# Moving a square root, eight scalings and four gathers in GpSimd's order

## The chip, the cores and the metric

The kernel runs on one core of a Trainium2 chip. Its time is the device time of one execution in microseconds (us). The engines are called PE (TensorE), DVE (VectorE), ACT (ScalarE), POOL (GpSimd) and SP (SyncE, which issues most DMAs). They run side by side and wait for one another by semaphores.

## The reference

One layer of a language model on `x` of 8 x 256 tokens with 256 features: `x + attention(layernorm(x)) + experts(layernorm(x))`, all in float32.

```python
# attention: 16 key heads, 32 value heads of 128; per value head and token
state = state * exp(g_t)
delta = (v_t - einsum('bhkv,bhk->bhv', state, k_t)) * b_t
state = state + einsum('bhk,bhv->bhkv', k_t, delta)
o = einsum('bhkv,bhk->bhv', state, q_t)
...
xg = out * silu(z)
y = xg * rsqrt(mean(xg * xg, axis=-1, keepdims=True) + RMS_EPS) * norm_w
return y.reshape(B, S, VDIM) @ w_out
# experts: 8 of 2048 rows for each of 8 heads and each token
de = down_embed[indices]
ue = up_embed[indices]
z = silu(einsum('btd,bthkd->bthk', h, de) * softmax(sc, axis=-1))
out = einsum('bthk,bthkd->btd', z, ue)
```

q, k and v come out of a projection, a causal convolution over 4 tokens and a silu.

## The kernel before

After a routing stage (some 280 us: layer norm, the search for each token's experts, the gates) the kernel makes 64 passes of some 45 us. A pass is one key head for 512 tokens (4 tiles of 128, two sequences of two chunks), 16 heads times 4 groups of tokens. Each pass works on two heads at once: the **front** of head n+1 (projections, convolution taps, silu, norms, the triangular matrices and the inversion of their 16x16 blocks) and the **back** of head n (levels that complete the inverse, the state, the outputs, the gate, the output projection of the head before). 8 value tasks of 128x128 make up one such pass. Beside that every pass treats 16 of a token's 64 experts for one tile: their 16 rows of 384 floats are gathered into `rows`.

All orders are written out by hand: every engine has a function `one_pass` whose sequence of calls is its program, and each call waits for semaphores. An engine that waits holds back whatever is written behind the waiting instruction. Nothing is moved by a scheduler.

POOL's pass (L961 to L986), in the order of before:

- `cols` and `xr` are copied (L971, L973), once the transfers that read the last `xr` and `xrT` are through;
- `gate_sums` (L944): `gn`, then 8 scalings of a mask into `gm` (L950), once PE has used the last ones (`diff_t`);
- `gather(f, 0)` (L958): 8 indirect DMAs of one row for each of 128 tokens, for k = 0 to 3 of two expert heads. They wait for `half_v`, by which DVE says that it has used those rows of the last tile;
- `finish` (L936): waits for `rms_v`, takes the power -0.5 of the 128x8 sums `rms` (L939), and scales the 8 tasks of `xg` by it (L942, each 128x128, `y_p` counted after each);
- the power for `norm` (L983), once DVE has written both halves of `ss` (`ssk_v`);
- `gather(f, 1)`: the other 8 DMAs, k = 4 to 7, once DVE has used the rows (`mix_v`).

Who uses these results: PE transposes the scaled `xg` in `finish_transposes` (L496), 4 tasks after each fourth `y_p`, between the product at L584 and the projection at L522. `norm` is read by ACT (L874) and DVE (L1148) in the next pass. The rows of the first half are read by DVE's dot products (L1201, `expert_dots(0)`) at the end of the pass, just before the addition at L1154, and by the mixing (L1216 to L1222) behind it; those of the second half by the same lines in the middle of the next pass. Between them DVE's pass has the taps (L1181), the masks on the levels (L1169), `rms` (L1136), `kq` and `MT` (L1290, L1298), the sum into `acc` (L1350) and the elimination in the blocks (L1234, L1238).

SP writes the inverted blocks to a scratch tensor in HBM (L362, L363) and reads them back as whole matrices, `X16` (L368) and `XT16` (L371). PE's first product of the next pass (L556) waits for the first, its product at L569 for the second.

Of the kernel before, what the change touches and what calls it, by code (L numbers as in the profile page):

```python
# [51 lines left out]
K = 8  # L52
# [27 lines left out]
def program(nc, x, wkq, wvz, ckq, cvv, woh, wba, dtb, alog, nw, wup, bup, wdn, bdn, wq, keys, table, consts, out):  # L80
    ctx = ExitStack()
    with ctx:
        def sb(name, shape, dt=F32):
            return ctx.enter_context(nc.sbuf_tensor(name, shape, dt))

        def sem(name):
            return ctx.enter_context(nc.semaphore(name))
# [7 lines left out]
        idx_all = sb("idx_all", [P, TILES, EH * K], U32)  # L95
# [26 lines left out]
        gathered = [sem(f"gathered{i}") for i in range(2)]  # L122
# [54 lines left out]
        def at(name, n):  # L177

            return place["u"] * per[name] + n

        def last(name, n=None):

            return (place["u"] - 1) * per[name] + (per[name] if n is None else n)
# [739 lines left out]
        def _(pool):  # L923
# [12 lines left out]
            def finish():  # L936

                pool.wait_ge(sm["rms_v"], at("rms_v", 1))
                pool.tensor_tensor(rms[:, :], rms[:, :], minus_half, ALU.pow).then_inc(sm["rms_p"], 1)  # L939
                pool.wait_ge(sm["rms_p"], at("rms_p", 1))  # L940
                for a in range(TASKS):
                    pool.tensor_scalar(xg[:, a, :], xg[:, a, :], rms[:, a:a + 1], None, ALU.mult).then_inc(sm["y_p"], 1)  # L942

            def gate_sums(f, calls=1):  # L944

                pool.tensor_copy(gn[:, :].rearrange("p (t r) -> p t r", t=4),  # L946
                                 gates[:, 3, bass.ds(4 * (f // HEADS), 4), bass.ds(R * (f % HEADS), R)]).then_inc(sm["gn_p"], 1)
                pool.wait_ge(sm["gn_p"], at("gn_p", calls))
                for a in range(TASKS):
                    pool.tensor_scalar(gm[:, a, :], mask(C_LE), gn[:, a:a + 1], None, ALU.mult).then_inc(sm["gm_p"], 1)  # L950

            def gather(f, hf):

                for k in range(hf * (K // 2), (hf + 1) * (K // 2)):
                    for s in range(2):
                        m = K * s + k
                        c = (f % 4) * 16 + m
                        pool.indirect_dma_start(rows[:, m, :], None, table[:, :],  # L958
                                                bass.IndirectOffsetOnAxis(ap=idx_all[:, f // 4, c:c + 1], axis=0)).then_inc(gathered[hf], 16)

            def one_pass(f, nx, n):  # L961

                if f is None:
                    finish()
                    return
                hn, pn = f % HEADS, f // HEADS
                if place["u"]:
                    pool.wait_ge(sm["qs_s"], last("qs_s"))
                    pool.wait_ge(sm["inv_out"], last("inv_out"))
                    pool.wait_ge(sm["invt_out"], last("invt_out"))  # L970
                pool.tensor_copy(cols2[nx][:, :, :].rearrange("p q (t r) -> p q t r", t=4),  # L971
                                 gates[:, 0:3, bass.ds(4 * pn, 4), bass.ds(R * hn, R)]).then_inc(sm["cols_p"], 1)
                pool.tensor_copy(xr[:, 0:BL * BL], cst[0:NB * TASKS, C_EYE * P:(C_EYE + 2) * P]).then_inc(sm["zero_p"], 1)  # L973
                pool.wait_ge(sm["diff_t"], at("diff_t", 2))
                if f + 1 < PASSES:
                    gate_sums(f + 1, 2 if n is None else 1)
                if n is not None:
                    pool.wait_ge(sm["half_v"], at("half_v", 1))
                gather(f, 0)
                if n is not None:  # L980
                    finish()
                pool.wait_ge(sm["ssk_v"], at("ssk_v", 2))
                pool.tensor_tensor(norm2[nx][:, :], ss[:, :, :].rearrange("p w t -> p (w t)"), both, ALU.pow).then_inc(sm["norm_p"], 1)  # L983
                if n is not None:
                    pool.wait_ge(sm["mix_v"], at("mix_v", 1))
                gather(f, 1)  # L986

            place["u"] = 0
            gate_sums(0)
# [7 lines left out]
            pool.memset(norm2[1][:, :], 0.0).then_inc(zeroed, 1)  # L997
            pool.wait_ge(zeroed, 7)
            one_pass(0, 0, None)
            end_pass(pool, 1)  # L1000
            for n in range(PASSES):
                place["u"] = n
                one_pass(n + 1 if n + 1 < PASSES else None, 1 - n % 2, n)
# [441 lines left out]
```

## Time and profile before

| | us |
|---|---|
| median of three runs | 3237.49 |
| lowest and highest | 3236.72, 3246.71 |
| the profiled execution | 3209.48 |
| its span, first to last instruction | 3207.7 |
| mean granted clock of TensorE in it | 0.975 of full speed |

The profile is one execution of the same program. Its own time is 28 us under the median of the others; sums below are made in the profiled execution and their result is added to the median. In the trace a group of equal instructions has one row, a start and a length in us from the start of the span; an instruction's idle time before it, and what ended it, stand in brackets.

### The profile page before, as it was taken

How to read it: one execution, taken by the hardware profiler on the slowest of the kernel's cores; microseconds unless marked ns; L12 is line 12 of the kernel's file. 1: busy time of each engine (PE TensorE's matmuls, PEld its weight loads, DVE VectorE, ACT ScalarE, POOL GpSimd, SP SyncE). 2: the span in 40 equal slices, each digit the busy share in tenths (PEclk: the TensorE clock that was granted, in tenths of full speed). 3: DMA queues.
4: the chain of work that ended last, by engine and by line, in shares of the span. 5: the costliest groups of instructions: out<-in, count | busy, mean ns of one | idle time of the engine just before them, and what ended most of it. 6: DMA issues, size and time to landing. Idle time of an engine off the chain costs nothing.

```text
span 3207.7 us, 56507 instructions
## 1 busy us (share of the span) xinstructions
PE 2926.0 (91%) x18444; PEld 2394.4 (75%) x18444; DVE 2951.7 (92%) x9293; ACT 1798.5 (56%) x4175; POOL 2218.9 (69%) x2394
## 2 busy tenths in 40 slices
PE   7942899999999999999999999999999999999997
PEld 4421678787878877878778877788787787877876
DVE  4997899999999999999999999999999999999996
ACT  3321555565556655565555655566555665656554
POOL 0003677877777777777777777787777777777764
PEclk9975999999999999999999999999999999999999
DMA  2002555555555555555555555555555565555653
GB/s 64 1 1 66 151 142 144 143 149 156 140 146 138 156 151 140 143 141 156 144 146 135 151 157 142 144 138 155 151 145 139 142 159 146 149 134 146 159 143 85
DMA packets 541829, 427.99 MB, mean 133 GB/s; under 512 B 247009, under 2 KB 450785, under 8 KB 541537
## 3 DMA queue, kind: packets, MB, share of 16 engines
q1 hardware_dynamic: 476000, 222.98, 25.6%
q0 software_dynamic: 65536, 201.39, 24.0%
q8 instruction: 149, 2.44, 0.3%
q14 instruction: 144, 1.17, 0.1%
HBM read 345.61 MB, written 45.09 MB: 122 GB/s over the span
## 4 chain that ended last, share of the span: by engine, by line
DVE 62%; PE 22%; ACT 8%; issue 5%; DMA 1%; POOL 1%; POOLq 1%; DVEq 0%; SPq 0%; ACTq 0%
DVE mix L1222 12%; DVE qkv L1181 9%; PE ps L584 4%; DVE E L1169 4%; DVE rows L1201 4%; PE ps L522 3%; DVE xg L1148 3%; PE ps L526 3%; PE ps L556 3%; PE ps L569 3%; PE ps L576 3%; DVE xr L1238 3%; ACT L824 2%; ACT L841 2%; DVE outer L1234 2%
## 5 line engine op out<-in xcount | busy, mean ns | idle before, releaser
L958 POOL DMA_INDIRECT rows<-table,idx_all x1024 | 1200.1, 1172 | 382.7 <-issue 280.3
L813 ACT ACTIVATE qkv<-qkv 128x512 f32<-128x512 f32 x256 | 161.4, 630 | 603.8 <-DVE qkv L1181 603.8
L942 POOL TENSOR_SCALAR xg<-xg,rms 128x128 f32<-128x128 f32 x520 | 407.3, 798 | 7.0
L576 PE MATMUL ps<-XT,E 128*128 128x128 f32 x3072 | 400.5, 277 | 0.0
L556 PEld LDWEIGHTS ps<-X,AT 128*128 128x128 f32 x3072 | 363.4, 192 | 35.7 <-DMA X<-whole 17.9
L1222 DVE SCALAR_TENSOR_TENSOR mix<-rows,zc,mix 128x256 f32<-128x256 f32 x896 | 381.3, 491 | 0.4 <-ACT zc L824 0.4
L556 PE MATMUL ps<-X,AT 128*128 128x128 f32 x3072 | 375.2, 275 | 3.3 <-DMA X<-whole 3.3
L576 PEld LDWEIGHTS ps<-XT,E 128*128 128x128 f32 x3072 | 368.7, 192 | 0.0
L946 POOL COPY gn<-gates 128x8 f32<-128x8 f32 x64 | 12.3, 193 | 481.3 <-SPq L330 262.2
L950 POOL TENSOR_SCALAR gm<-cst,gn 128x128 f32<-128x128 f32 x512 | 340.3, 680 | 6.5
L808 ACT ACTIVATE raw<-ps 128x512 f32<-128x512 f32 x256 | 152.9, 597 | 313.5 <-PE ps L522 313.5
L1181 DVE SCALAR_TENSOR_TENSOR qkv<-raw,cwkq,qkv 128x510 f32<-128x510 f32 (+2 forms) x384 | 287.5, 749 | 31.0 <-ACT qkv L809 12.5
L569 PEld LDWEIGHTS ps<-E,XT 128*128 128x128 f32 x2048 | 262.4, 194 | 64.5 <-issue 64.3
L1181 DVE SCALAR_TENSOR_TENSOR qkv<-raw,cwv,qkv 128x510 f32<-128x510 f32 (+2 forms) x384 | 285.4, 743 | 6.8
L1169 DVE TENSOR_TENSOR E<-ps,cst 128x512 f32<-128x512 f32 x384 | 257.2, 686 | 35.4 <-PE ps L556 32.1
L569 PE MATMUL ps<-E,XT 128*128 128x128 f32 x2048 | 272.8, 277 | 0.0
L827 ACT ACTIVATE XT<-ps 128x512 f32<-128x512 f32 x384 | 228.1, 594 | 77.5 <-PE ps L576 70.5
L522 PE MATMUL ps<-xnT,Wkq 128*128 128x512 f32 x512 | 259.1, 630 | 6.2 <-DVE km L1272 0.5
L505 PE MATMUL ps<-wo,yT 128*128 128x256 f32 x1040 | 246.9, 381 | 0.0
L1201 DVE CUSTOM_DVE_ANT_0 rows<-rows,h_all 128x128 f32<-128x128 f32 x1024 | 239.3, 295 | 7.0 <-SPq L330 7.0
L522 PE MATMUL ps<-xnT,Wvz 128*128 128x512 f32 x512 | 242.7, 597 | 0.0
L526 PE MATMUL ps<-Wvz,xb 128*128 128x256 f32 x1024 | 241.9, 379 | 0.0
(165 smaller groups left out, 6172.5 us busy)
## 6 DMA issues: line engine op xcount, KB each, us to landing
Wvz<-wvz SPq DMA_DIRECT2D x64, 512.0 KB, 3.2
xb<-xnT SPq DMA_DIRECT2D x64, 512.0 KB, 4.5
whole<-AT SPq DMA_DIRECT2D x128, 256.0 KB
X<-whole SPq DMA_DIRECT2D x128, 256.0 KB, 4.2
XT<-whole SPq DMA_DIRECT2D x128, 256.0 KB, 4.7
wo<-woh SPq DMA_DIRECT2D x65, 256.0 KB, 4.4
Wkq<-wkq SPq DMA_DIRECT2D x64, 256.0 KB, 2.9
rows<-table,idx_all POOLq DMA_INDIRECT x1024
```

The costliest lines, as they stand in the source:

```text
L522: done = mm(ps[:, bank, :], w[:, k, :], xnT[:, k, bass.ds(pn * N, N)], start=k == 0, stop=k == KD - 1)
L526: done = mm(ps[:, bank, (t % 2) * 256:(t % 2) * 256 + 256], xb[:, k, t * P:(t + 1) * P], Wvz[:, k, 2 * P:4 * P], start=k == 0, stop=k == K ...
L556: done = mm(ps[:, g, (a % 4) * P:(a % 4 + 1) * P], AT_b[:, a, :], src[:, a, :], start=True, stop=True)
L569: done = mm(ps[:, 2 + g, (a % 4) * P:(a % 4 + 1) * P], src[:, a, :], E[:, a, :], start=True, stop=True)
L576: done = mm(ps[:, 4 + g, (a % 4) * P:(a % 4 + 1) * P], E[:, a, :], src[:, a, :], start=True, stop=True)
L942: pool.tensor_scalar(xg[:, a, :], xg[:, a, :], rms[:, a:a + 1], None, ALU.mult).then_inc(sm["y_p"], 1)
L950: pool.tensor_scalar(gm[:, a, :], mask(C_LE), gn[:, a:a + 1], None, ALU.mult).then_inc(sm["gm_p"], 1)
L958: pool.indirect_dma_start(rows[:, m, :], None, table[:, :], bass.IndirectOffsetOnAxis(ap=idx_all[:, f // 4, c:c + 1], axis=0)).then_inc(ga ...
L1169: V.tensor_tensor(E[:, 4 * g:4 * g + 4, :], ps[:, g, :].rearrange("p (a i) -> p a i", a=4), mask(C_MS + lv, 4), ALU.mult)\
L1181: ins = V.scalar_tensor_tensor(out=o, in0=i, scalar=w, in1=o, op0=ALU.mult, op1=ALU.add)
L1201: st.did(V.tensor_tensor_reduce(out=rows[:, k, 0:P], in0=rows[:, k, 0:P], in1=h2_all[:, n // 4, :], scale=1.0, scalar=0.0, op0=ALU.mult, o ...
L1222: sums[s] = st.did(V.scalar_tensor_tensor(out=mix[:, s, :], in0=rows[:, m, P:ROW], scalar=zc[:, 1, m:m + 1], in1=mix[:, s, :], op0=ALU.mul ...
```

## The change

Only the order of POOL's instructions changes. `gather` takes a range of k in place of a half, and adds to the semaphore of the half that k belongs to, so that both halves are counted as before. The first half is issued in two parts: four gathers (k = 0, 1) ahead of `finish`, four (k = 2, 3) behind it and ahead of `norm`.

```diff
-            def gather(f, hf):
+            def gather(f, k0, k1):
 
-                for k in range(hf * (K // 2), (hf + 1) * (K // 2)):
+                for k in range(k0, k1):
                     for s in range(2):
...
-                                                bass.IndirectOffsetOnAxis(ap=idx_all[:, f // 4, c:c + 1], axis=0)).then_inc(gathered[hf], 16)
+                                                bass.IndirectOffsetOnAxis(ap=idx_all[:, f // 4, c:c + 1], axis=0)).then_inc(gathered[k // 4], 16)
...
-                gather(f, 0)
+                gather(f, 0, 2)
                 if n is not None:
                     finish()
+                gather(f, 2, 4)
                 pool.wait_ge(sm["ssk_v"], at("ssk_v", 2))
...
-                gather(f, 1)
+                gather(f, 4, 8)
```

POOL in a pass of the loop before, from the first gather to the next pass's copy. Names in brackets are the semaphores that an instruction waits for.

```order
L958 DMA rows<-table,idx_all 128x384 [waits half_v]
L958 DMA rows<-table,idx_all 128x384 x7
L939 TENSOR_TENSOR rms<-rms,powers 128x8 [waits rms_v]
L942 TENSOR_SCALAR xg<-xg,rms 128x128 [waits rms_p]
L942 TENSOR_SCALAR xg<-xg,rms 128x128 x7
L983 TENSOR_TENSOR norm<-ss,powers 128x8 [waits ssk_v]
L958 DMA rows<-table,idx_all 128x384 [waits mix_v]
L958 DMA rows<-table,idx_all 128x384 x7
L971 COPY cols<-gates 128x24 [waits invt_out,inv_out,qs_s]
```

All eight gathers of the first half stand ahead of the power. The same stretch now:

```order
L958 DMA rows<-table,idx_all 128x384 [waits half_v]
L958 DMA rows<-table,idx_all 128x384 x3
L939 TENSOR_TENSOR rms<-rms,powers 128x8 [waits rms_v]
L942 TENSOR_SCALAR xg<-xg,rms 128x128 [waits rms_p]
L942 TENSOR_SCALAR xg<-xg,rms 128x128 x7
L958 DMA rows<-table,idx_all 128x384 x4
L984 TENSOR_TENSOR norm<-ss,powers 128x8 [waits ssk_v]
L958 DMA rows<-table,idx_all 128x384 [waits mix_v]
L958 DMA rows<-table,idx_all 128x384 x7
L971 COPY cols<-gates 128x24 [waits invt_out,inv_out,qs_s]
```

Four gathers have moved from ahead of the power to behind the last scaling. The other engines' orders are the same in both kernels. DVE's in the middle of a pass, which POOL waits for and runs beside (line numbers of the changed kernel, one more than before; `ISA` is a dot product):

```order
L1137 TENSOR_SCALAR rms<-sumsq 128x8 [waits sumsq_s]
L1182 SCALAR_TENSOR_TENSOR qkv<-raw,cwkq,qkv 128x2x255 [waits tap_s]
L1182 SCALAR_TENSOR_TENSOR qkv<-raw,cwkq,qkv 128x2x254 [waits step_v]
L1182 SCALAR_TENSOR_TENSOR qkv<-raw,cwkq,qkv 128x2x253 [waits step_v]
L1170 TENSOR_TENSOR E<-ps,cst 128x512 [waits e_t] x2
L1202 ISA rows,dot<-rows,h_all 128x128 [waits gathered1]
```

Nothing moved here: `rms` stands ahead of three taps, two masks and the eight dot products of the second half.

## Rows read from the trace of the kernel before

**Rows 1.** The page: busy time by engine, and the chain's shares by engine.

```profile
PE 2926.0 (91%) x18444; PEld 2394.4 (75%) x18444; DVE 2951.7 (92%) x9293; ACT 1798.5 (56%) x4175; POOL 2218.9 (69%) x2394
...
DVE 62%; PE 22%; ACT 8%; issue 5%; DMA 1%; POOL 1%; POOLq 1%; DVEq 0%; SPq 0%; ACTq 0%
```

**Rows 2.** The chain in order of time: start, us, what.

```profile
1519.59 1.80 PE ps L556 x16
1521.42 0.69 DVE E L1169
```

**Rows 3.** Timeline of POOL in one pass: start, us, engine, line, operation, [idle before].

```profile
1509.09 1.46 POOL L958 DMA_INDIRECT rows<-table,idx_all  x1 [1.17 <-DVEq L1322]
...
1514.86 0.95 POOL L958 DMA_INDIRECT rows<-table,idx_all  x1 [0.31 <-issue]
...
1520.83 1.69 POOL L939 TENSOR_TENSOR rms<-rms,powers 128x8 f32<-128x8 f32 x1
1522.63 6.37 POOL L942 TENSOR_SCALAR xg<-xg,rms 128x128 f32<-128x128 f32 x8
1528.97 1.66 POOL L983 TENSOR_TENSOR norm<-ss,powers 128x8 f32<-128x8 f32 x1
1530.80 1.08 POOL L958 DMA_INDIRECT rows<-table,idx_all  x1 [0.17 <-issue]
...
1541.29 1.39 POOL L958 DMA_INDIRECT rows<-table,idx_all  x1 [0.31 <-issue]
...
1542.96 0.39 POOL L973 COPY xr<-cst 64x256 f32<-64x256 f32 x1
1546.82 0.19 POOL L946 COPY gn<-gates 128x8 f32<-128x8 f32 x1 [3.47 <-PE ps L532]
```

**Rows 4.** Timeline of the same pass, DVE.

```profile
1500.54 0.28 DVE L1201 CUSTOM_DVE_ANT_0 rows<-rows,h_all 128x128 f32<-128x128 f32 x1
...
1502.24 0.08 DVE L1201 DVE_READ_ACCUMULATOR2_ANT dot<- 128x1 f32 x1
...
1511.14 0.87 DVE L1148 SCALAR_TENSOR_TENSOR xg<-QS,norm,z 128x256 f32<-128x256 f32 x2
...
1518.39 0.16 DVE L1136 TENSOR_SCALAR rms<-sumsq 128x8 f32<-128x8 f32 x1
...
1522.03 0.28 DVE L1201 CUSTOM_DVE_ANT_0 rows<-rows,h_all 128x128 f32<-128x128 f32 x1
...
1523.89 0.08 DVE L1201 DVE_READ_ACCUMULATOR2_ANT dot<- 128x1 f32 x1
...
1526.06 3.39 DVE L1222 SCALAR_TENSOR_TENSOR mix<-rows,zc,mix 128x256 f32<-128x256 f32 x8
```

**Rows 5.** Waits of PE in the whole span (us, times, longest), then its timeline.

```profile
PEld ps L496 <- POOL xg L942: 9.8, 42, 1.5
...
1532.20 1.16 PE L584 MATMUL ps<-E,Kd 128*128 128x128 f32 x8 [0.77 <-DVE E L1307]
```

**Rows 6.** Waits for X16; timelines of two passes around PE's first product and the mixing.

```profile
PEld ps L556 <- DMA X<-whole: 17.9, 43, 1.9
...
1501.97 1.86 PEld L556 LDWEIGHTS ps<-X,AT 128*128 128x128 f32 x16 [0.58 <-DMA X<-whole]
...
1505.38 0.49 DVE L1216 SCALAR_TENSOR_TENSOR mix<-rows,zc,acc 128x256 f32<-128x256 f32 x1 [0.63 <-ACT zc L824]
...
1321.39 0.74 PEld L556 LDWEIGHTS ps<-X,AT 128*128 128x128 f32 x6 [0.99 <-DMA X<-whole]
...
1324.38 0.49 DVE L1216 SCALAR_TENSOR_TENSOR mix<-rows,zc,acc 128x256 f32<-128x256 f32 x1 [0.21 <-ACT zc L824]
```

**Rows 7.** DMA: the gathers' queue; one stretch by windows (last: DMA share, GB/s); landing of XT16.

```profile
q0 software_dynamic: 65536, 201.39, 24.0%
...
1540.70:1542.70 2.00, 1.90 (x14) 1.45 (x13) 1.97 (x5) 2.00 (x9) 1.69 (x3) 1.00 1.01 131
...
XT<-whole SPq DMA_DIRECT2D x128, 256.0 KB, 4.7
```

## The prediction, written before the changed kernel ran

> **What bounds the kernel now.** I read the page first: engine shares, then the chain. DVE is busy for 92% of the span and PE for 91%; DVE has 62% of the chain, PE 22%, POOL 1% [rows 1]. So POOL, the only engine whose program changes, does not set the end now. It can matter in three ways: by what it hands over (the scaled `xg`, `norm`, `gm`, gathered rows), by what it costs DVE to run beside it, and by when its gathers load the DMA engines. Next I read the chain in order of time for one pass. It is the same in the passes I compared. In the middle of a pass it is PE's levels until 1521.42, then DVE without a break through the mask, the second half's dot products, the mixing and the elimination [rows 2, 4]. Last I read the timeline of POOL beside those of DVE and PE. POOL works without a hole from 1509.09 to 1543.35 (the end of the copy at L973). It is idle 3.47 us before `gn` and 1.17 us before the first gather, 4.64 us of 44.55 [rows 3].
>
> **What the change does on POOL.** `rms` is ready at 1518.39 + 0.16 = 1518.55 [rows 4], but POOL takes it up at 1520.83, since eight gathers are in front of it: 2.28 us late [rows 3]. Now the fourth gather ends at about 1514.6 (the fifth starts at 1514.86) and POOL idles until 1518.6, some 4 us. From there, with the durations of [rows 3]:
> - power 1.69, a gap of 0.11 and scalings 6.37: `xg` is finished at 1526.8, where it was 1529.0. 2.2 us earlier.
> - gathers five to eight: they took from 1514.86 to the power at 1520.83, 5.97 us. Now 1526.8 to 1532.8.
> - `norm` with its gap, 1.83 us: starts at 1532.8 in place of 1528.97, ends at about 1534.6.
> - second half: 1530.80 to 1542.68 were 11.88 us. Now 1534.6 to 1546.5. Each of them comes 3.7 to 3.8 us later.
> - two copies, 0.67 us: done at 1547.2, 0.4 us after the moment (1546.82) at which `gn` could start. Of the 1.17 us before the next first gather 0.8 are left, so the delay does not grow from pass to pass. POOL has no more than this: if its work turns out over 0.8 us slower in a pass, the gathers and with them all that follows on POOL slip from pass to pass.
>
> **Who gains.** Only PE waits for the scaled `xg`: 42 times, 9.8 us together, 0.2 us on average [rows 5]. This wait goes. What is late next is DVE: after the transposes and one projection PE stands 0.77 us until DVE has scaled Y [rows 5], and that is in DVE's own unbroken row. So the 0.2 us become more waiting there, and I count **0**. If DVE were no longer late there, the cover would be gone and the term would be at most 9.8 us.
>
> **Who is handed things later.** `norm` is read in the next pass, some 20 us on. The rows of gathers five to eight must be there for the dot products at 1500.54 + 44.55 = 1545.1; issued by 1532.8, they have 12 us. The second half, issued by 1546.5, is read at 1522.03 + 44.55 = 1566.6. `gm`, 0.4 us late, is used by PE a whole pass later; the copied `xr` 27 us later. All **0**, by covers of 12 us or more.
>
> **What POOL costs DVE.** This is the only term on the chain. Eight dot products with POOL idle run from 1500.54 to 1502.24; beside the scalings the same eight take from 1522.03 to 1523.89 [rows 4]. 1.86 - 1.70 = 0.16 us. The scalings are 0.80 us each, so some two fell in that time: 0.08 us each. For the mixing I have the same form (three operands, 128x256) at L1148 beside gathers: two in 0.87 with 0.48 for one, a step of 0.39. Eight mixing steps by that are 0.48 + 7 x 0.39 = 3.21 to 3.25 us, and they took 3.39 [rows 4]: 0.14 us for four scalings beside them. Now the scalings run from 1518.6 + 1.8 = 1520.4 to 1526.8:
> - dot products, 1522.0 to 1523.9: three scalings in place of two, +0.08. Bounds: 0 (two, as now) and +0.32 (each of the three costs twice what the two did).
> - mixing, 1526.06 to 1529.5: one scaling in place of four, gathers beside the rest, which cost L1148 nothing: -0.11. Bounds: -0.14 and 0, if gathers cost the mixing what scalings did.
> - taps and first mask, 1518.47 to 1521.4: the power and the first scaling in place of gathers. The chain is PE's until 1521.42 [rows 2], so a few hundredths are covered. +0.01, bounds 0 and +0.08.
> - `gm`, up to 0.4 us later, overlaps more of the next pass's mixing: +0.05, bounds -0.1 and +0.11 (as one more overlap of the size above, or one less).
>
> Sum +0.03 us for each of 63 passes (all of the loop but the last, which gathers nothing): **+2 us**. The ends add up to -0.24 and +0.51, thus -15 and +32 us; I take the middle since each bound is an extreme of its own.
>
> Here a rule can be weighed. What the rows show: a DVE instruction with two inputs in SBUF loses 0.04 to 0.08 us to a scaling beside it, never a scaling's whole length of 0.80 us [rows 3, 4]. The Trainium skill, "SBUF — State Buffer", section "Who interferes with whom", has the port pair shared by VectorE and GpSimd as an exclusive lock, on which the one that comes second blocks for the other's whole instruction. By that, four overlaps in place of six would give back 1.6 us a pass; by the rows, hundredths.
>
> **What the later gathers do to other transfers.** X16 is read from 1540.7 on, in a stretch where the DMA engines are taken up (share 1.01) [rows 7]. The gathers' queue has 24.0% of 3207.7 us for 1024 gathers, 0.75 us of all engines each [rows 7]. Now the last gathers are issued until 1546.5 in place of 1542.7, so one more of them may fall ahead of the end of X16: between 0 and two gathers, 0 to 1.5 us; I take half a gather, 0.4. Its cover: when PE waited 0.58 us for X16, DVE still idled 0.63 us for ACT ahead of the mixing; at a wait of 0.99 it idled 0.21 [rows 6]. So DVE is hit from a wait of 1.20 us on. The waits are 17.9 us in 43 passes, 0.42 on average [rows 6], which leaves 0.8 us. At +0.4: **0**. XT16 lands 4.7 us after issue [rows 7], about 2 us before it is used, and may lose 1 us of that.
>
> **Sum.** In the profiled execution 3209.5 + 2; on the median 3237.5 + 2 = **3239.5 us**.
>
> **The rivals.**
> - *Slower by X16.* The moved gathers hold X16 back by more than its cover. It decides from +0.8 us. At +1.1 us it costs 0.3 x 63 = 19 us: 3257. For it: full DMA engines at 1540.7. Against: the same number of gathers goes at the same pace, and only one or two change sides. 0.08. The Trainium skill, "DMA: Bandwidth & Descriptors", section on one DMA's anatomy ("Arbitration"), has each engine alternate between queues by packets, so that gathers take turns with X16 and don't wait behind it; that would put the delay near the upper end.
> - *Slower by DVE.* The scalings fall squarely on the dot products (+0.2) and `gm` gets one more overlap (+0.1), while the mixing gains less: about +0.25 us a pass, 16 us, 3253. It decides where the net cost passes 0.15 us. 0.11.
> - *Faster by DVE.* The mixing gains its 0.14, `gm` 0.1, and the dot products lose nothing, -0.24 x 63: 3222. 0.11.
> - *Faster by the lock.* If overlaps really cost whole instructions and the trace's small numbers hide it: two fewer of 0.80 us, 1.6 x 63 = 101 us, 3137. The rows of DVE speak against it. 0.01.
> - That the change doesn't do what it says I exclude: the built order of POOL shows it, and both semaphores of the gathers are counted as before.
>
> **How the numbers follow.** My forecast (nothing on the path, a few hundredths on DVE) has 0.69. 0.3% is 9.7 us, about what a measurement of this kernel can tell from no change. Faster by more: the two faster cases, 0.12. Slower by more: the two slower ones, 0.19. The rest, 0.69, is within. The range goes from 3225 to 3256: it takes in the forecast's own 3229 to 3247 and the nearer half of each rival with an ordinary price.
>
> **What would show it.** In the changed profile: POOL idle some 4 us ahead of L939, taken up within 0.1 us of `rms`; no idle time left, or under 0.5 us, ahead of `gn` (it was 3.5); some 0.8 us ahead of the first gather. PE's waits for `xg` at L496 gone, and the wait at L584 for DVE longer by as much. The eight dot products longer than 1.86 us, the eight mixings shorter than 3.39. Waits for X16 longer, still under 1.2. I am wrong if passes change by more than 0.15 us: then either the first product waits over 1.2 us for X16, or DVE's rows differ by more than hundredths, or something waits for POOL that I called covered.

## The result: 0.5% faster, and the profile after

| | before | after |
|---|---|---|
| median | 3237.49 (7 runs, 3234.20 to 3246.71) | 3223.46 (7 runs, 3215.29 to 3228.56) |
| ratio, 95% interval | | 0.9948 [0.9931, 0.9964] |
| the profiled execution | 3209.48 | 3227.67 |
| mean granted clock in it | 0.975 | 0.971 |

The changed kernel is faster by 0.5%. The prediction said no change that can be measured, 3239.5 us, and its range began at 3225. The table shows the riddle: by the medians the change gains 14 us, by the two profiled executions it loses 18. The page after, where [rows 1] were:

```profile
PE 2938.9 (91%) x18444; PEld 2401.1 (74%) x18444; DVE 2955.6 (92%) x9293; ACT 1799.2 (56%) x4175; POOL 2168.7 (67%) x2394
...
DVE 52%; PE 30%; ACT 8%; issue 6%; DMA 1%; POOL 1%; POOLq 1%; SPq 0%; DVEq 0%; ACTq 0%
```

One pass of POOL after, where [rows 3] were. It runs from 1243.68 to 1288.31; code lines behind L979 have moved by one.

```profile
1250.15 1.47 POOL L958 DMA_INDIRECT rows<-table,idx_all  x1 [1.17 <-DVEq L1323]
...
1259.64 2.10 POOL L939 TENSOR_TENSOR rms<-rms,powers 128x8 f32<-128x8 f32 x1 [4.04 <-DVE rms L1137]
1261.85 5.90 POOL L942 TENSOR_SCALAR xg<-xg,rms 128x128 f32<-128x128 f32 x8
1267.92 1.23 POOL L958 DMA_INDIRECT rows<-table,idx_all  x1 [0.17 <-issue]
...
1273.13 1.68 POOL L984 TENSOR_TENSOR norm<-ss,powers 128x8 f32<-128x8 f32 x1
1275.00 1.40 POOL L958 DMA_INDIRECT rows<-table,idx_all  x1 [0.19 <-issue]
...
1285.39 0.95 POOL L958 DMA_INDIRECT rows<-table,idx_all  x1 [0.30 <-issue]
...
1286.52 0.45 POOL L973 COPY xr<-cst 64x256 f32<-64x256 f32 x1
1287.97 0.26 POOL L946 COPY gn<-gates 128x8 f32<-128x8 f32 x1 [1.00 <-PE ps L532]
```

POOL idles 4.04 us ahead of the power. The second half begins at 31.3 us of the pass and its last gather at 41.7. DVE in that pass and the next, where [rows 4] were:

```profile
1263.08 0.45 DVE L1202 CUSTOM_DVE_ANT_0 rows<-rows,h_all 128x128 f32<-128x128 f32 x1
...
1265.11 0.08 DVE L1202 DVE_READ_ACCUMULATOR2_ANT dot<- 128x1 f32 x1
...
1267.28 3.28 DVE L1223 SCALAR_TENSOR_TENSOR mix<-rows,zc,mix 128x256 f32<-128x256 f32 x8
...
1286.65 0.47 DVE L1202 CUSTOM_DVE_ANT_0 rows<-rows,h_all 128x128 f32<-128x128 f32 x1
```

And the waits over the span, where [rows 5, 6] were (us, times, longest):

```profile
PEld ps L556 <- DMA X<-whole: 18.8, 41, 1.9
PE ps L496 <- POOL xg L942: 8.6, 2, 7.5
PEld ps L569 <- DMA XT<-whole: 7.7, 13, 1.2
```

The state product of this pass in the timeline of PE:

```profile
1273.32 1.16 PE L584 MATMUL ps<-E,Kd 128*128 128x128 f32 x8 [1.02 <-DVE E L1308]
```

PE's 42 short waits for `xg` at L496 [rows 5] are down to one of 1.5 us; the two long ones of the rows above are as before. All this is close to what was foretold, and it can't gain 14 us.

### The profile page after: what moved, and what is told of

Its sections match the earlier page's. It is cut to its first block, busy times and chain, and to the rows that moved or that the text cites. A ratio compares the mean times of both kernels' runs of the same rounds, so it can differ in the third digit from the quotient of the medians.

```text
span 3225.9 us, 56507 instructions
## 1 busy us (share of the span) xinstructions
PE 2938.9 (91%) x18444; PEld 2401.1 (74%) x18444; DVE 2955.6 (92%) x9293; ACT 1799.2 (56%) x4175; POOL 2168.7 (67%) x2394
## 3 DMA queue, kind: packets, MB, share of 16 engines
q14 instruction: 143, 1.17, 0.1%
## 4 chain that ended last, share of the span: by engine, by line
DVE 52%; PE 30%; ACT 8%; issue 6%; DMA 1%; POOL 1%; POOLq 1%; SPq 0%; DVEq 0%; ACTq 0%
DVE mix L1223 11%; DVE qkv L1182 8%; PE ps L522 5%; PE ps L556 4%; PE ps L569 4%; PE ps L584 4%; DVE rows L1202 4%; PE ps L576 4%; PE ps L526 3%; DVE xr L1239 3%; DVE outer L1235 2%; PE ps L539 2%; ACT L824 2%; ACT L841 2%; DVE prod L1245 2%
## 5 line engine op out<-in xcount | busy, mean ns | idle before, releaser
L958 POOL DMA_INDIRECT rows<-table,idx_all x1024 | 1151.0, 1124 | 359.3 <-issue 273.1
L576 PE MATMUL ps<-XT,E 128*128 128x128 f32 x3072 | 400.4, 277 | 0.0
L556 PEld LDWEIGHTS ps<-X,AT 128*128 128x128 f32 x3072 | 362.7, 192 | 36.3 <-DMA X<-whole 18.8
L942 POOL TENSOR_SCALAR xg<-xg,rms 128x128 f32<-128x128 f32 x520 | 378.7, 742 | 7.0
L576 PEld LDWEIGHTS ps<-XT,E 128*128 128x128 f32 x3072 | 368.8, 192 | 0.0
L939 POOL TENSOR_TENSOR rms<-rms,powers 128x8 f32<-128x8 f32 x65 | 131.5, 2023 | 283.6 <-DVE rms L1137 283.6
L569 PEld LDWEIGHTS ps<-E,XT 128*128 128x128 f32 x2048 | 262.9, 194 | 69.1 <-issue 61.2
L1170 DVE TENSOR_TENSOR E<-ps,cst 128x512 f32<-128x512 f32 x384 | 256.7, 685 | 36.2 <-PE ps L556 25.4
L569 PE MATMUL ps<-E,XT 128*128 128x128 f32 x2048 | 274.1, 277 | 1.3 <-DMA XT<-whole 1.3
L1202 DVE CUSTOM_DVE_ANT_0 rows<-rows,h_all 128x128 f32<-128x128 f32 x1024 | 257.2, 311 | 7.1 <-SPq L330 7.1
```

Source lines behind the costliest of these rows:

```text
L556: done = mm(ps[:, g, (a % 4) * P:(a % 4 + 1) * P], AT_b[:, a, :], src[:, a, :], start=True, stop=True)
L569: done = mm(ps[:, 2 + g, (a % 4) * P:(a % 4 + 1) * P], src[:, a, :], E[:, a, :], start=True, stop=True)
L576: done = mm(ps[:, 4 + g, (a % 4) * P:(a % 4 + 1) * P], E[:, a, :], src[:, a, :], start=True, stop=True)
L958: pool.indirect_dma_start(rows[:, m, :], None, table[:, :], bass.IndirectOffsetOnAxis(ap=idx_all[:, f // 4, c:c + 1], axis=0)).then_inc(ga ...
L1170: V.tensor_tensor(E[:, 4 * g:4 * g + 4, :], ps[:, g, :].rearrange("p (a i) -> p a i", a=4), mask(C_MS + lv, 4), ALU.mult)\
L1202: st.did(V.tensor_tensor_reduce(out=rows[:, k, 0:P], in0=rows[:, k, 0:P], in1=h2_all[:, n // 4, :], scale=1.0, scalar=0.0, op0=ALU.mult, o ...
```

## What two traces of the kernel before show

The measure that I use from here on is the time from one addition into `QS` on DVE (L1154) to the next. Its median over the passes that no stretch of halved clock touches is called the typical pass. It is 44.56 us in the first trace of before, 44.62 in that of after, and **44.85** in a second trace of before (e1, span 3241.5). So the first trace was not like the executions of which the median tells. The difference lies between 14 and 20 us of the pass. ACT there in the first trace of before; it copies what PE has made at L569 and L576:

```profile
1518.74 0.60 ACT L827 ACTIVATE X<-ps 128x512 f32<-128x512 f32 x1 [0.30 <-PE ps L569]
1519.63 0.60 ACT L827 ACTIVATE XT<-ps 128x512 f32<-128x512 f32 x1 [0.30 <-PE ps L576]
```

The same place in e1, all engines:

```profile
1534.64 1.06 PE L569 MATMUL ps<-E,XT 128*128 128x128 f32 x8
...
1535.53 1.06 PE L576 MATMUL ps<-XT,E 128*128 128x128 f32 x8
...
1536.57 0.60 ACT L827 ACTIVATE X<-ps 128x512 f32<-128x512 f32 x1 [0.90 <-PE ps L569]
1536.62 1.21 POOL L958 DMA_INDIRECT rows<-table,idx_all  x1 [0.31 <-issue]
1537.85 1.69 POOL L939 TENSOR_TENSOR rms<-rms,powers 128x8 f32<-128x8 f32 x1
1538.02 0.60 ACT L827 ACTIVATE XT<-ps 128x512 f32<-128x512 f32 x1 [0.85 <-PE ps L576]
...
1538.11 1.29 DVE L1169 TENSOR_TENSOR E<-ps,cst 128x512 f32<-128x512 f32 x2 [0.33 <-PE ps L556]
```

PE's products start at their usual pace, but ACT gets the second one 1.4 us later than it should (1538.02, when PE started it at 1535.53; in the first trace 1519.63 and 1518.54). The mask on DVE is late too, and the pass is 0.3 us longer. I call this **held**: PE has made a result, and the engine that waits for it is let go late, here by over half a microsecond. The copy is held in 49 of 61 passes of e1 (in all 48 that no halved clock touches), in none of the first trace, and in none of after.

## The experiments

The expectations name theories by letters. In those of e1 and e2, **A** says that the first trace of before was unlike its other executions, and **B** that this was chance (e1) or that the gain is one of fewer stretches of halved clock (e2). In those of e3 to e6, **S** says that the gain comes from PE's results between 14 and 20 us, which are late in the kernel before because of the gathers beside them, and **D** that it comes from where the scalings of `xg` lie beside DVE's work. Later texts say what they mean. The table gives for each kernel the order on POOL (numbers are gathers, f the power and scalings, n `norm`, p an added scaling of 128x128), the time and its ratio to the kernel before beside it; then, out of one trace, the typical pass, the passes of 61 in which a copy was held at 14 to 20 us, or the state product at 38 to 44 us, the stretches of halved clock in the loop, and how many of the 16384 landings of gathers the trace has a record of.

| | order | us | ratio [95%] | typical | held 14-20 | held 38-44 | halved | records |
|---|---|---|---|---|---|---|---|---|
| before, first trace | 8 f n 8 | 3209.5 | | 44.56 | 0 | 0 | 7 | 100% |
| e1 | 8 f n 8 | 3239.6 | 1.0005 [0.9993, 1.0017] | 44.85 | 49 | 0 | 13 | 58% |
| e13 | 8 f n 8 | 3239.2 | one run | 44.85 | 49 | 0 | 14 | 57% |
| after | 4 f 4 n 8 | 3223.5 | 0.9948 [0.9931, 0.9964] | 44.62 | 0 | 10 | 10 | 71% |
| e2 | 4 f 4 n 8 | 3219.8 | 0.9947 [0.9928, 0.9966] | 44.63 | 0 | 9 | 9 | 71% |
| e14 | 4 f 4 n 8 | 3217.7 | 0.9937 [0.9916, 0.9958] | 44.55 | 0 | 9 | 9 | 72% |
| e18 | 4 f 4 n 8 | 3219.6 | 0.9949 [0.9931, 0.9967] | 44.63 | 0 | 8 | 9 | 71% |
| e3 | 4 f n 4 8 | 3339.6 | 1.0315 [1.0286, 1.0344] | 44.69 | 0 | 51 | 52 | 51% |
| e4 | 4, f late, 4 n 8 | 3254.4 | 1.0043 [1.0014, 1.0073] | 44.62 | 0 | 2 | 12 | 58% |
| e5 | 6 f 2 n 8 | 3238.8 | 1.0001 [0.9986, 1.0016] | 44.98 | 0 | 46 | 13 | 57% |
| e6 | 8 f n 8, AT late | 3239.2 | 1.0003 [0.9990, 1.0016] | 44.83 | 54 | 0 | 9 | 58% |
| e7 | small p 8 f n 8 | 3400.6 | 1.0424 [1.0394, 1.0454] | 46.99 | 61 | 0 | 56 | 43% |
| e8 | p 8 f n 8 | 3405.2 | 1.0433 [1.0405, 1.0461] | 47.28 | 61 | 0 | 33 | 42% |
| e9 | 6 f 2 n p 8 | 3231.1 | 0.9912 [0.9881, 0.9942] | 44.83 | 11 | 0 | 12 | 65% |
| e10 | 4 f 4 n p 8 | 3238.5 | 0.9918 [0.9889, 0.9947] | 44.84 | 0 | 0 | 13 | 73% |
| e11 | 6 p 2 f n 8 | 3233.7 | 0.9987 [0.9974, 1.0001] | 44.83 | 2 | 46 | 13 | 52% |
| e12 | p 6 f 2 n 8 | 3232.3 | 0.9984 [0.9972, 0.9996] | 44.83 | 48 | 45 | 13 | 55% |
| e15 | 6 p 2 f n p 8 | 3211.4 | 0.9992 [0.9977, 1.0007] | 44.55 | 0 | 0 | 8 | 100% |
| e16 | p 8 f n 8 | 3205.4 | one run | 44.55 | 0 | 0 | 6 | 100% |
| e17 | 6 p 2 f n 6 p 2 | 3209.8 | 0.9982 [0.9969, 0.9996] | 44.55 | 0 | 0 | 6 | 100% |

The kernel before took 3237 to 3241 us beside most of them, but 3261.2 us beside e7 to e10 and 3216.3 us beside e15 to e17. By the record's chip numbers e1 and e2 ran on chip 6, e3 to e6 and e15 to e17 on chip 12, e7 to e10 on chip 3, e11 to e14 and e18 on chip 1. The typical pass of e3 is that of 10 passes and that of e7 of 7, since halved clock touches the others.

**e1 and e2: both kernels again.**

> The kernel before, unchanged, profiled a second time. The profiled execution on which the prediction rested took 3209.5 us, 28 us under the median of the others. Theory A (that execution was unlike the others): this profile takes some 3237 us, and its passes differ from the 44.55 us of the first trace, by a lower granted clock in more stretches (some 14 more of them at 2 us each) or by another course of the pass. Theory B (chance, the trace was representative): again within a few us of 3210.

> The changed kernel, unchanged, profiled a second time. Theory A (only the first profile of the kernel before was unlike its other runs): 3215 to 3229 us, passes of 44.62 us, some 10 passes with a half-speed stretch, as in its first trace. Theory B (the gain is one of fewer half-speed stretches): their number is smaller here than in the second profile of the kernel before by some 7.

Both times came again, 3239.6 and 3219.8. What did not is the profiled 3209.5 of before. So theory A holds. By passes the gap of the two spans, 3241.5 to 3225.9, is accounted for: 61 times 0.23 us are 14 us. What the 61 passes take beyond 61 typical ones is 22 us in e1 and 20 in after, though after has three stretches of halved clock fewer, because one costs more there. The first and last passes and what follows them give 3 us, and after's loop began 3 us later. So theory B of e2 accounts for some 2 of the 16 us. Two such runs can't say why the copies are held.

**e3 and e4: other places for `norm` and for the power.**

```diff
-                gather(f, 2, 4)
                 pool.wait_ge(sm["ssk_v"], at("ssk_v", 2))
                 pool.tensor_tensor(norm2[nx][:, :], ...)
+                gather(f, 2, 4)
```

> The changed kernel with the power for norm back where it was, behind the scalings, and gathers five to eight behind it. Both theories have the same for this place: the gain is in what left the stretch ahead of rms, so 3220 us within 0.3%. If it is not (3237), the place of norm matters, which neither has.

```diff
                 gather(f, 0, 2)
                 if n is not None:
+                    pool.wait_ge(sm["e_v"], at("e_v", 5))
                     finish()
```

> The changed kernel, but the power of rms waits for DVE's first mask of level 2, 19.0 us into a pass of 44.6, so the scalings run as late as in the kernel before (from some 20.8 to 27.2 us), while gathers five to eight stay behind them. Theory S (stretch: in the usual executions of the kernel before, PE's signals come late between 14 and 19 us of a pass, since gathers five to eight are issued there beside the writes of AT, and the pass takes 44.88 in place of 44.56 us): passes of 44.6 to 44.7 us, 3220 to 3226 us, no late signals. Theory D (the scalings' place beside DVE: mixing freed of them): the gain goes, 3237 us.

e3 took 3339.6 us, a surprise. Its trace is of an execution of 3379.7 us, where the others took 3328.5 to 3348.6, so its counts may be high for the others. No copy was held at 14 to 20 us, but the state product at the end of the second half was, by 1.8 us, in 51 passes; and there were 52 stretches of halved clock, one in each of these passes. In the ten passes without a stretch it is late by 0.4 us at most. The row of the held product among the waits of the whole span ("remote": the profile finds no signal that fits):

```profile
DVE E L1308 <- remote: 92.0, 52, 1.9
```

In e4 the power comes at 19.0 us of the pass (18.4 in e1), and nothing is held at 14 to 20 us, where POOL now idles. So it is not the late power that holds. It is not faster, though, and its time is outside what either theory said. Its gathers run beyond the end of the pass, and the first mask of the next pass (L1170) was held 0.75 us in 50 passes. Its typical pass hides this: 19 of the 49 passes without halved clock take over 45.3 us. The scalings lie 0.6 us later than in e1, and the held copies are gone all the same. The time of e4 doesn't decide on theory D. What speaks against D is the first trace of before: where no copy is held, the old order has a typical pass of 44.56 us, no longer than after's.

**e5: six gathers ahead of the power, two behind it.**

```diff
-                gather(f, 0, 2)
+                gather(f, 0, 3)
...
-                gather(f, 2, 4)
+                gather(f, 3, 4)
```

> Six gathers ahead of the power and two behind, in place of four and four. Gathers five and six are then issued at 12.4 to 15.1 us of a pass, the scalings still begin when rms is there (some 17.9 us). Theory S: the late signals begin at 14 to 15 us with the sixth and seventh gather; with only one of these left between none and half of the 0.3 us comes back, 3220 to 3230 us. Theory D: as the changed kernel, 3220 us.

It is no faster than before, and again nothing is held at 14 to 20 us. Now the state product is held, in 46 passes. One of them, all engines:

```profile
1696.68 1.16 PE L584 MATMUL ps<-RV,XT 128*128 128x128 f32 x8 [0.18 <-DVE RV L1378]
1696.72 1.39 POOL L958 DMA_INDIRECT rows<-table,idx_all  x1 [0.30 <-issue]
...
1698.69 0.76 DVE L1308 TENSOR_TENSOR E<-ps,scol 128x256 f32<-128x256 f32 x2 [0.62 <-PE ps L584]
```

DVE starts 2.01 us behind the product; in after it is 1.30 (1101.65 and 1102.95). The last gather of the second half started 0.04 us behind the product, ended at 1698.11, and 0.6 us later DVE went on.

**e6: the order of before, AT written later.** On SP, ahead of the writes of AT:

```diff
+                if b is not None:
+                    sp.wait_ge(sm["rms_p"], at("rms_p", 1))
```

> The kernel before with POOL's order unchanged; SP writes AT only after the power of rms (20 us into a pass in place of 14 and 16), so that these writes no longer lie beside gathers five to eight. Theory S in the form that both together are needed: no late signals between 14 and 19 us, passes of 44.6 us and 3221 to 3226 us, if the blocks still come back in time (they land at 22 us now, some 26.5 then, and DVE needs them at 27.4). Theory S in the form that the gathers alone do it: signals late as before, 3237 us or more. Theory D: 3237 us.

Held in 54 passes, with the first write of AT issued at 20.4 us of a pass. So the writes of AT that run beside these products do not hold them.

**e7 to e10: a pad ahead of the gathers.** `spare` is a tile that nobody reads.

```diff
                     pool.wait_ge(sm["half_v"], at("half_v", 1))
+                    pool.tensor_scalar(spare[:, 0:128], mask(C_LE)[:, 0:128], powers[:, 0:1], None, ALU.mult)
                 gather(f, 0)
```

e8 is this; e7 has 16 in place of 128 columns; e9 and e10 have it ahead of the second eight gathers, e9 with the order of e5, e10 with that of after.

> The kernel before with one scaling of a 128x16 piece into a spare tile added on GpSimd ahead of the first gather of a pass, so that the eight gathers and the scaling of xg behind it all move by about 0.15 us and nothing else of the order changes. Theory S (TensorE's results at 15 to 19 us of a pass are reported late, by up to 1.4 us, when GpSimd's last gathers of the first half meet them at a certain distance): a shift so small may break the meeting, 3222 to 3225 us with no late copy in the typical pass, or leave it, 3239. Rival N (the late reports come with eight gathers ahead of the scaling in any place): 3239 to 3242 us and late copies in nearly all of the passes.

> The same with a 128x128 scaling, about 0.6 us. Theory S, exact distance: gathers 7 and 8 then start at 16.0 and 17.8 us of the pass in place of 15.4 and 17.2; the typical pass falls by 0.3 us, less up to 0.3 us because xg, which TensorE already waited for in 42 passes, comes 0.6 us later: 3222 to 3240 us, with few late copies. Rival N: late copies in nearly all passes and xg late on top, 3245 to 3275 us.

> Six gathers ahead of the scaling and two behind it, as in the run of 3238.8 us, with a 0.6 us scaling into a spare tile ahead of the second eight gathers. There the state product at 38.4 us of the pass was reported 0.65 us late in 34 of 35 undisturbed passes, beside the last gather of the second eight. Theory S: with that gather 0.6 us later (39.0 us) the report is on time, the typical pass is 44.6 us and the time 3218 to 3226 us. Rival N (six and two is slower by its order): 3239 us again and the state product late in the same passes.

> The changed kernel with the same 0.6 us ahead of the second eight gathers. GpSimd then waits 0.4 us in place of 1.0 us at the copy for the sums of the gates. Theory S gives two cases: no meeting at the new distance, 3220 to 3226 us; or a new meeting, late reports in most passes at some place and 3235 to 3245 us. Rival C (what was left of GpSimd's spare time was what kept it fast): gn, gm and the first gather later by up to 0.1 us, 3226 to 3232 us.

e7 and e8 came out 130 us and more above all expectations. One pass of e8 at the place in question, in order of time:

```profile
1316.42 1.06 PE L577 MATMUL ps<-XT,E 128*128 128x128 f32 x8
...
1317.10 0.60 ACT L828 ACTIVATE X<-ps 128x512 f32<-128x512 f32 x1 [0.20 <-PE ps L570]
...
1317.31 1.06 PE L570 MATMUL ps<-E,XT 128*128 128x128 f32 x8
1317.86 0.96 POOL L959 DMA_INDIRECT rows<-table,idx_all  x1 [0.30 <-issue]
...
1318.20 1.06 PE L577 MATMUL ps<-XT,E 128*128 128x128 f32 x8
1319.10 1.06 PE L557 MATMUL ps<-X,AT 128*128 128x128 f32 x8
1319.12 1.21 POOL L959 DMA_INDIRECT rows<-table,idx_all  x1 [0.30 <-issue]
1320.35 1.68 POOL L940 TENSOR_TENSOR rms<-rms,powers 128x8 f32<-128x8 f32 x1
1321.41 0.60 ACT L828 ACTIVATE XT<-ps 128x512 f32<-128x512 f32 x1 [3.71 <-remote]
1321.69 0.69 DVE L1171 TENSOR_TENSOR E<-ps,cst 128x512 f32<-128x512 f32 x1 [1.40 <-remote]
```

Four results were made from 1316.42 on. None was handed over until 1321.4, 1.1 us behind the end of the last gather. Then all came, and ACT copied one after the other. This gives theory **H**: the results of PE are held while POOL issues one gather after another, and are let go when the series ends or pauses. It fits where the held results were let go: over all passes the held copy of e7 and e8 came 1.1 us behind the end of the last gather, that of e1 0.2 to 0.3 us, the held product of e3 and e5 0.5 and 0.6 us. In e9 the last gather of the second half starts 1.7 us behind the state product in place of 0.04, and the product was on time (0 passes, 46 in e5). The forecast made of it, 3218 to 3226 us and a pass of 44.6, failed all the same: 3231.1 and 44.83, and no run shows what took the rest. Both e9 and e10 are faster than the kernel before beside them, by 0.9 and 0.8%; of that kernel there is no trace from this occasion. e10 lost after's spare time at `gn` (idle 0 us), has a typical pass of 44.84 with nothing held at either place, and at 3238.5 us lies above all that was said for a case without held results.

H is too broad as it stands. In after's typical pass the state product starts 3.9 us ahead of the end of the series, in its midst, and is on time; in the passes with halved clock it starts 1.4 us ahead of it and is held in 10 of 10. What was held started in the last 3.9 us of a series (e8), and not everything that did was held: in e3 the product starts 2.7 us ahead of the end and is held, in e9 it does too and is not. In e1 it lies beside the last gather just as in e5, and is handed over 1.31 us after its start:

```profile
1558.56 1.16 PE L584 MATMUL ps<-RV,XT 128*128 128x128 f32 x8
1558.60 1.39 POOL L958 DMA_INDIRECT rows<-table,idx_all  x1 [0.30 <-issue]
...
1559.87 0.42 DVE L1307 TENSOR_TENSOR E<-ps,scol 128x256 f32<-128x256 f32 x1
```

**e11 and e12: the same pad as a pause, and the pad without gathers 7 and 8.**

```diff
+                gather(f, 0, 3)
+                    pool.tensor_scalar(spare[:, 0:128], mask(C_LE)[:, 0:128], powers[:, 0:1], None, ALU.mult)
+                gather(f, 3, 4)
                     finish()
```

This is e11. In e12 the scaling stands ahead of `gather(f, 0, 3)`, and `gather(f, 3, 4)` behind `finish()`.

> The order of before (eight gathers, then the scaling of xg), with one 0.6 us scaling into a spare tile between the sixth and the seventh gather of the first half. The same work stood ahead of the first gather in the run of 3405 us, where the copies of TensorE's results waited up to 3.7 us and went on about 1.1 us behind the end of GpSimd's last gather. Theory H (results of TensorE are held back while GpSimd issues gather after gather, and come when that series ends or pauses): the pause lets the held results through near 15 us of the pass, the typical pass is 44.6 to 45.1 us, 3222 to 3255 us. Rival P (the spare tile or the added instruction itself makes such a pass long, wherever it stands): 3380 to 3410 us again. Rival L (only the later xg costs, as far as it is later): 3240 to 3265 us, without late copies.

> The 0.6 us scaling ahead of the first gather as in the run of 3405 us, but the seventh and eighth gather stand behind the scaling of xg. Theory H: without gathers at 15 to 18 us of the pass there is nothing to hold TensorE's results back there, so the copies come on time; second eight gathers as in the six-and-two order, where the state product was held 0.65 us at the end of the second half or not at all: 3218 to 3245 us. Rival P: 3380 to 3410 us.

> The kernel before once more, for one more profile. Theory H with two states of the same kernel: late copies in nearly all undisturbed passes and a typical pass near 44.87 us, since 37 of 37 timed runs on the first chips lie at 3231 to 3247 us; a pass of 44.56 us, as in the first profile, would come with a time near 3210 us.

> The changed kernel once more, on whichever chip this is. Theory H: its results of TensorE are on time in the typical pass (44.62 us), ratio 0.990 to 0.997 to the kernel before. Rival (the gain hangs on the chip): a ratio of 0.999 or more on this one.

In e11 the held copies went from 49 passes to 2. One pass of it:

```profile
1613.88 1.40 POOL L959 DMA_INDIRECT rows<-table,idx_all  x1 [0.30 <-issue]
...
1614.95 0.61 PE L577 MATMUL ps<-XT,E 128*128 128x128 f32 x4
...
1615.32 0.79 POOL L982 TENSOR_SCALAR spare<-cst,powers 128x128 f32<-128x128 f32 x1
...
1615.77 0.60 ACT L828 ACTIVATE XT<-ps 128x512 f32<-128x512 f32 x1 [0.29 <-PE ps L577]
```

The copy comes in the pause, 0.5 us behind the end of the sixth gather. The rivals P and L fall: 3233.7 us, with the same instruction in it that stood in e8. The state product is now held (46 passes). H alone can't explain this: the second half is an unbroken series of eight, and the product has the place beside its last gather that it has in e1 and e13, where it is on time in every pass. In e12 the expectation by H was copies on time, and they are held in 48 passes, until 1.0 us behind the *sixth* gather, with the rest behind the scalings: again they are let go behind the series' end, wherever it is. e13 found before as e1 had, e14 the gain of after a third time.

**e15 to e18: two pauses, e8's kernel again, and after once more.**

```diff
+                    pool.tensor_scalar(spare2[:, 0:128], mask(C_LE)[:, 0:128], powers[:, 0:1], None, ALU.mult)
                 gather(f, 4, 8)
```

This is e15, on top of e11. e17 has the same scaling between `gather(f, 4, 7)` and `gather(f, 7, 8)`.

> The order of before with the 0.6 us pause between the sixth and seventh gather, and the same again ahead of the second eight gathers. The pause alone gave 3233.7 us: no late copies at 15 to 19 us, but the state product at 40.3 us of the pass 0.65 us late in 46 passes, where the last gather of the second half starts at 38.2 us. Theory H: 0.6 us later (38.9 us, about as in before, where that product is on time) both are on time, the typical pass is 44.2 to 44.5 us, 3195 to 3218 us, faster than both kernels. Rival E (what is not held in one place is lost at another: the end of the pass is set by the copy for gates and the first products of the next): 3225 to 3240 us with no held result.

> The kernel of the run of 3405 us once more (0.6 us ahead of the first gather, eight gathers, then the scaling), on the chip of the others, since that run and the one with the pause were made on two chips. Theory H: the results of TensorE are held until the series of gathers ends again, 3380 to 3405 us. Rival (the chip made it): 3235 to 3260 us.

> The pause between the sixth and the seventh gather of the first eight, and one of the same length between the last two gathers and the six ahead of them in the second eight. Theory H: the state product's report falls into the second pause or behind the last gather at 38.9 us; no held result, 3195 to 3218 us. Rival E: 3225 to 3240 us with no held result. If the pause is passed before the product is done (it ends near 39.6 us), the product is held 0.6 us or more again and the time is 3233 us or more.

> The changed kernel a last time. Beside e15 to e17 no result of TensorE was held and the kernel before took 3216 us in place of 3238 us. If that is so here too, theory H (the gain is only that the changed order escapes the hold) expects no gain: the typical pass was 44.56 us before and 44.62 us after, so 3217 to 3222 us against 3216 us, a ratio of 0.999 to 1.002. If results are held here, before is at 3238 us and the ratio 0.992 to 0.996 as at the other times. Rival (the changed order is faster by itself): a ratio of 0.995 in either.

e15 and e17 gave the times that H foretold, and prove nothing for it: beside them the kernel before took 3216.3 us, and e16, the kernel of the 3405 us, took 3205.4 in a single run, outside both of its forecasts. Nothing was held in any of the three traces. One pass of e16, to be set beside that of e8:

```profile
1244.46 1.06 PE L577 MATMUL ps<-XT,E 128*128 128x128 f32 x8
...
1245.55 0.60 ACT L828 ACTIVATE XT<-ps 128x512 f32<-128x512 f32 x1
1245.89 0.95 POOL L959 DMA_INDIRECT rows<-table,idx_all  x1 [0.31 <-issue]
...
1246.44 0.60 ACT L828 ACTIVATE X<-ps 128x512 f32<-128x512 f32 x1 [0.30 <-PE ps L570]
1247.14 1.21 POOL L959 DMA_INDIRECT rows<-table,idx_all  x1 [0.30 <-issue]
1247.34 0.60 ACT L828 ACTIVATE XT<-ps 128x512 f32<-128x512 f32 x1 [0.30 <-PE ps L577]
```

The same gathers at the same pace beside the same products. ACT copies 1.1 us behind each product (1244.46 and 1245.55); in e8 it was 5.0 us (1316.42 and 1321.41). So a series of gathers is not enough for a hold. A further condition belongs to the single occasion and not to the chip alone: on chip 12 results were held in e3 to e6, and none in e15 to e17. The last column of the table goes with it: in the four traces that have a record of at least 99.8% of the landings nothing is held. In the sixteen others 27 to 58% of the records are missing, and there results are held in fifteen; e10 alone shows none at these two places. In e18 the kernel before was back at 3241.0 us, the time that it has where results are held, and after had its gain a fourth time. The changed kernel was never run where nothing is held.

## Why the prediction was wrong

- **The step that failed is in the sum**: "In the profiled execution 3209.5 + 2; on the median 3237.5 + 2." The 28 us between the two were taken for an offset that any order of POOL would have. Of the 33.8 us between the spans of the two traces of before (3207.7 and 3241.5), 61 times 0.29 = 18 are the typical pass with its held copies, 7 the passes that six more stretches of halved clock touch, and 6 lie ahead of the loop; the rest is in other single passes. The change is just what removes the held copies. The first trace had no row of this, but the 28 us stood in the table. A trace 0.9% away from the runs whose median is to be forecast is of another kind of execution, and it can't be the base for a difference of 0.1%.
- **Against the executions of its own kind the sum was right**: +0.03 us a pass was foretold, 44.56 to 44.62 is +0.06, and the four traces of after have 44.55 to 44.63. 3216.3 us for before where nothing is held and 3219.6 for after are 3 us apart; they were not taken side by side, and e18 has its state product held in 8 passes.
- **Terms.** POOL idles 4.04 us (said: some 4) and takes `rms` up at once. The last scaling of `xg` ends at 24.1 us of the typical pass in place of 26.6, 2.5 us earlier where 2.2 were said: the power takes 2.10 in place of 1.69, and the eight, which lie beside less of the mixing, 5.90 in place of 6.37. The short waits at L496 went and the one at L584 grew from 0.77 to 1.02. The dot products went from 1.86 [rows 4] to 2.03, +0.17 where +0.08 was said (bound 0.32). The mixings went from 3.39 to 3.28, -0.11 as said. The second half comes 2.9 us later, not 3.7, so 1.0 us of idle time is left ahead of `gn` (0 foretold) and all of the 1.17 ahead of the first gather.
- **X16**: 18.8 us in 41 passes after 17.9 in 43 [rows 6]. The later gathers cost it nothing measurable. They cost XT16 its margin in 13 passes, 7.7 us together (no such wait in the first trace of before), where the prediction had it land about 2 us ahead of its use and lose 1 us of that. (The rule of arbitration that the prediction cites from the Trainium skill, "DMA: Bandwidth & Descriptors", stands there in the section "Queues, rings and completion order"; these waits don't tell whether it holds here.)
- **Overlooked**: the copy at L973 now falls on a dot product, which takes 0.47 in place of 0.28 us. The 0.19 us are given back at the start of the next pass, where DVE waits less for ACT and PE.
- **The rivals.** "Faster by DVE" has the time (3222) and is not the cause; DVE lost a little. The lock rule of the Trainium skill ("SBUF — State Buffer", "Who interferes with whom") can be weighed once more: the dot product beside the 0.45 us copy lost 0.19 us, less than the copy's length, and dot products of after beside scalings of some 0.7 us took 0.36 and 0.45 us in place of 0.28.

What is shown: in fifteen traces results of PE near the end of a series of gathers are handed over late, mostly only when the series has ended, the place moves with the series (e3, e4, e5, e12), with a pause in the first series the copies are on time (held in 49 passes of e13 and 2 of e11, on one chip), and the changed order has no held copy between 14 and 20 us, which is 14 of the 16 us between e1 and after. What stays open: what holds them, which results near the end of a series are held and which are not, and why nothing is held in four traces.

The Trainium skill, "NOTIFIC — the notification-queue block", section 7.1, has the block that writes trace records, when a queue is full, by one setting or another either drop new ones or stall the engine that makes them. If something of both kinds is at work here, a hold would go with missing records, and the gain would be one of recorded executions. That is a guess: no run here shows the kernel without records, so it is not tested. The Trainium skill, "Perfetto Trace Analysis", section "Tensor Engine Instruction (MATMUL, LD_WEIGHTS)", has PE's end as an estimate and its signal as pushed only once the last bytes are written; the rows agree in so far as PE's rows look alike in e8 and e16, and only the waits of the others tell.

## What to carry to other kernels

Before anything is summed up, set the profiled execution's time beside the median. If they differ by more than the change can be worth, the profile's own gaps must be found first, by another profile of the same kernel; count records too. And where another engine waits for a result that was made long ago, see what GpSimd is issuing at that moment. A pause in its series of gathers, or another split of it, moved the held results here in every run that had one, and was worth up to 0.9% (e9; 0.5% in after). Often they only turned up at another place, and where nothing was held such a change was worth 0.2% at most (e15, e17).

## What the runs showed of the hardware

- A result of TensorE was handed over up to 3.9 us late while GpSimd issued gathers, in all 61 passes of e8, and the same kernel showed nothing of it in e16: 3405 and 3205 us, on chips 3 and 12.
- The clock halves for 3.4 us in 6 to 14 passes of 64, mostly near 12 us of a pass, but in 52 passes of e3, 56 of e7 and 33 of e8. In e1 (length, busy us of PE, PEld, DVE, ACT and POOL, the granted clock, the DMA engines' share, GB/s):

```profile
666.50:669.90 3.40, 2.34 (x19) 2.10 (x19) 3.28 (x8) 2.91 (x11) 2.79 (x3) 1.00 0.51 132
670.00:673.38 3.38, 3.38 (x6) 1.41 (x5) 3.28 (x11) 0.15 (x1) 2.56 (x3) 0.50 0.53 164
```

PE's rows in this stretch, and the same four products in a pass at full clock:

```profile
669.68 3.51 PE L522 MATMUL ps<-xnT,Wkq 128*128 128x512 f32 x4
...
1531.04 1.98 PE L522 MATMUL ps<-xnT,Wkq 128*128 128x512 f32 x4
```

PE had been busy for 2.34 of 3.40 us at 2.4 GHz; at 1.2 GHz the same four products take 3.51 in place of 1.98 us, and such a pass is 1.4 us longer than the typical one in e1, 1.8 in the first trace of before and 2.3 in after. In after the later state product of such a pass falls near the end of the series and is held, in 10 of 10; in e1 it is the other way round, and 12 of the 13 such passes have no held copy. Where results are held by 1.8 us or more (e3, e7, e8) these stretches come in half of the passes or more. In e3 the stretch lies ahead of the hold in each pass; whether a hold brings the next stretch is not shown.
- A pad of 16 columns and one of 128 moved the second gather alike, to 9.19 and 9.21 us of the pass from 8.43: what an instruction ahead of a gather adds is not its own length alone.
